# Second layer's attention values: from f32 products and key sums to three f16 products of halves, in a new order

## The reference

```python
latent_kv = x @ w_kv_down                       # rank 128
k, v = split(latent_kv @ w_kv_up); q = x @ w_q
att = softmax(where(causal, q k^T / 8, -inf))   # per head, 512 keys
y = einsum('bhqk,bkhd->bqhd', att, v)
return y.reshape(...) @ w_out
```

## Time and profile before

| | |
|---|---|
| runs shown | 3177.04, 3189.1, 3196.51 us (median 3189.1) |
| profiled execution | 3176.99 us, span 3175.3 us |
| busy share of the span | PE 94%, DVE 71%, ACT 56%, POOL 41% |
| granted TensorE clock, mean | 0.987 of 2.4 GHz |

### The profile page before, as it was taken

The page is one execution under the profiler, slowest core; times in us unless marked ns, Lnnn a source line. Parts: engine busy times, 40 slices in busy tenths (PEclk is TensorE's granted clock), DMA queues, the critical chain, the costliest instruction groups (busy, mean ns, idle before and its releaser), DMA issues.

```text
span 3175.3 us, 62002 instructions
## 1 busy us (share of the span) xinstructions
PE 2998.4 (94%) x22724; PEld 1597.1 (50%) x22724; DVE 2243.0 (71%) x4069; ACT 1765.3 (56%) x3674; POOL 1316.9 (41%) x1223
## 2 busy tenths in 40 slices
PE   4999999999999995799999999999999999999997
PEld 2565555555555553344444444444444444444443
DVE  4666666666666663787787787778778778878774
ACT  2666666665566664555555555555555555555543
POOL 1333333333333331354545545545544554455453
PEclk9999999999999998899999999999999999999998
DMA  4222222222222222434444445444444444453442
GB/s 119 51 53 51 51 51 56 64 56 63 51 51 51 62 50 83 110 100 117 128 113 123 116 115 135 111 112 126 115 121 112 128 126 104 125 135 100 124 121 67
DMA packets 271901, 297.58 MB, mean 94 GB/s; under 512 B 30832, under 2 KB 235760, under 8 KB 271088
## 3 DMA queue, kind: packets, MB, share of 16 engines
q1 hardware_dynamic: 249936, 276.88, 34.2%
q10 hardware_dynamic: 21664, 16.73, 1.7%
HBM read 141.46 MB, written 25.69 MB: 53 GB/s over the span
## 4 chain that ended last, share of the span: by engine, by line
PE 50%; DMA 3%; DVE 3%; issue 2%; SPq 2%; ACT 1%; POOL 0%; DVEq 0%; ACTq 0%; POOLq 0%
PE l_ps_out L1569 8%; PE l_ps_any L1469 6%; PE l_ps_any L1471 6%; PE l_ps_any L1470 6%; PE l_ps_any L1594 5%; PE l_ps_exp L1552 4%; PE l_ps_exp L1554 4%; PE l_ps_any L1601 4%; PE l_ps_any L1527 3%; DMA l_y_rec<-rec_scratch 2%; PE l_ps_sum L1580 2%; PE l_ps_exp L1556 2%; SPq L1099 1%; DVE l_neg_max L1392 1%; PE l_ps_any L1532 1%
## 5 line engine op out<-in xcount | busy, mean ns | idle before, releaser
L614 DVE TENSOR_REDUCE neg_max<-ps_any 128x1 f32<-128x384 f32 (+3 forms) x704 | 417.7, 636 | 264.0 <-PE ps_any L728 259.5
L1186 POOL TENSOR_TENSOR l_hid<-l_hid,l_spread 128x512 f32<-128x512 f32 x256 | 328.3, 1282 | 652.0 <-DVE l_hid L1421 481.1
L1273 ACT ACTIVATE l_probs<-l_ps_exp 128x512 f32<-128x512 f32 x640 | 376.8, 595 | 212.3 <-PE l_ps_exp L1556 201.8
L501 ACT ACTIVATE probs<-ps_exp 128x512 f32<-128x512 f32 x640 | 349.2, 602 | 151.5 <-PE ps_exp L743 150.8
L442 POOL TENSOR_SCALAR_AFFINE_SELECT probs<-probs 128x512 f32<-128x512 f32 x256 | 160.0, 637 | 591.1 <-ACT probs L501 591.1
L1392 DVE TENSOR_REDUCE l_neg_max<-l_ps_any 128x2 f32<-128x768 f32 (+2 forms) x384 | 316.3, 863 | 36.1 <-PE l_ps_any L1532 35.1
L1552 PE MATMUL l_ps_exp<-l_q_a,l_k_a 128*128 128x512 f16 (+3 forms) x1024 | 306.4, 300 | 10.0 <-DMA l_q_b<-l_max_row 6.3
L1569 PE MATMUL l_ps_out<-l_probs,l_v 128*64 128x512 f32 (+3 forms) x2048 | 303.9, 439 | 0.7 <-ACT l_yT L1248 0.7
L1425 DVE TENSOR_TENSOR l_hw<-l_hid,l_hw 128x512 f16<-128x512 f32 x272 | 258.6, 955 | 59.4 <-ACT l_hw L1256 58.9
L1554 PE MATMUL l_ps_exp<-l_q_b,l_k_b 65*128 65x512 f16 (+3 forms) x1024 | 295.3, 300 | 0.0
L1279 ACT ACTIVATE l_hid<-l_ps_any 128x512 f32<-128x512 f32 x272 | 162.4, 597 | 234.8 <-PE l_ps_any L1471 217.5
(11 more groups left out here) (233 smaller groups left out, 6514.4 us busy)
## 6 DMA issues: line engine op xcount, KB each, us to landing
l_spread<-route_scratch SPq DMA_DIRECT2D x128, 512.0 KB, 4.7
l_q_a<-l_q_hi SPq DMA_DIRECT2D x256, 128.0 KB, 2.4
l_y_rec<-rec_scratch SPq DMA_DIRECT2D x128, 256.0 KB, 4.3
l_q_b<-l_q_lo SPq DMA_DIRECT2D x128, 128.0 KB, 2.4
l_k_a<-l_k_hi SPq DMA_DIRECT2D x128, 128.0 KB, 3.0
l_k_a<-l_k_lo SPq DMA_DIRECT2D x128, 128.0 KB, 2.7
l_k_b<-l_k_hi SPq DMA_DIRECT2D x128, 128.0 KB, 2.7
q_st<-rot_hi SPq DMA_DIRECT2D x64, 128.0 KB
```

The source lines that it names most:

```text
L501: nc.scalar.activation(probs[:, n % 2, u], ps_exp[:, (10 * g + u) % 3], ACT.Exp, scale=float(HD0 + DR) ** -0.5).then_inc(exp_done.sem, 1)
L614: nc.vector.tensor_reduce(neg_max[:, n % 2, heads[0]:heads[0] + k, t], src, AX.X, ALU.max, negate=True).then_inc(drained["dve"], 1)
L1186: nc.gpsimd.tensor_tensor(at, at, spread[:, c % 3, n % SPREAD], ALU.mult).then_inc(weighted.sem, 1)
L1273: nc.scalar.activation(probs[:, n % 2, u], ps_exp[:, (5 * p + u) % ST_BANKS], ACT.Exp, scale=float(HD1) ** -0.5).then_inc(exp_done.sem, 1)
```

## The change

- Probabilities: for each unit ACT takes the exponential of the bank twice, to f16 (`probs` part 0) and to f32 (`p_in`, three slots); POOL subtracts, to f16 (`probs` part 1). The bank is free after the second. The scores get a constant added (`P_SHIFT` times `SHIFT` in a further row of the factors), and v a factor `V_SCALE`, which ACT takes out again.
- v: ACT writes the f16 hi half, DVE the lo half (`low_part`), and the bank is now counted as emptied by DVE.
- `values`: per key block three f16 products (hi*hi, hi*lo, lo*hi) for each of the two heads.
- `key_sum` and its POOL steps are gone. `sums` multiplies ones (f16) with both halves of the probabilities: 28 products a pair. Which queries share a row group of `ps_sum` changes (`HALVES`: blocks 0 and 3, 1 and 2), and `divide` becomes two instructions.
- `ORDER1` is another order of the same steps.

Unchanged lines are left out but for one ahead of each edit, and indents are cut; of the old order one line stands.

```diff
@@ -825,7 +825,11 @@
 XW, LW = X_SCALE * W_SCALE, LAT_SCALE * W_SCALE
-K_B = HD1 + 1
+K_B = HD1 + 2
+P_SHIFT = 0.13
+V_SCALE = 16.0
+P_SLOTS = 3
+HALVES = ((0, 3), (1, 2))
@@ -844,40 +848,40 @@
 ORDER1 = (
-    ("v", 0, 2, 0), ("rec", -1, 1), ("sums", -1, 7), ("exp", 0, 0, 4), ("v", 0, 3, 0), ("exp", 0, 1, 0),
...
+    ("spread_in", 0, 3), ("max", 0, 1, 1), ("exp", 0, 1, 0), ("max", 0, 1, 2), ("exp", 0, 1, 1),
+    ("max", 0, 1, 3), ("hw", 0, 4), ("rec_in", -1, 2), ("exp", 0, 1, 2), ("max", 0, 1, 4), ("hw", 0, 5),
+    ("values", 0, 0), ("exp", 0, 1, 3), ("up_in", 0, 6), ("exp", 0, 1, 4), ("turn_max", 0, 1), ("qk", 0, 2, 0),
+    ("qk", 0, 2, 1), ("gate_in", 0, 7), ("qk", 0, 2, 2), ("sums", 0, 0), ("divide", -1, 4), ("spread_in", 0, 4),
+    ("qk", 0, 2, 3), ("hw", 0, 6), ("v", 0, 0, 1), ("exp", 0, 2, 0), ("spread_in", 0, 5), ("rec_in", -1, 3),
+    ("max", 0, 2, 0), ("exp", 0, 2, 1), ("up_in", 0, 7), ("divide", -1, 5), ("down", 0, 0), ("exp", 0, 2, 2),
+    ("gate_in", 0, 8), ("hw", 0, 7), ("max", 0, 2, 1), ("down", 0, 1), ("up_in", 0, 8), ("max", 0, 2, 2),
+    ("gate_in", 0, 9), ("divide", -1, 6), ("values", 0, 1), ("max", 0, 2, 3), ("divide", -1, 7),
+    ("exp", 0, 2, 3), ("exp", 0, 2, 4), ("sums", 0, 1), ("norm", 1), ("spread_in", 0, 6), ("up_in", 0, 9),
+    ("gate_in", 0, 10), ("exp", 0, 3, 0), ("max", 0, 2, 4), ("exp", 0, 3, 1), ("load", 1), ("sums", 0, 2),
+    ("up_in", 0, 10), ("gate_in", 0, 11), ("turn_max", 0, 2), ("spread_in", 0, 7), ("up_in", 0, 11),
+    ("exp", 0, 3, 2), ("scale", 1), ("hw", 0, 8), ("out", -1, 1), ("v", 0, 1, 1), ("qk", 0, 3, 0),
+    ("v", 0, 2, 1), ("xnT", 1), ("hw", 0, 9), ("exp", 0, 3, 3), ("hw", 0, 10), ("qk", 0, 3, 1),
+    ("gate_in", 0, 12), ("exp", 0, 3, 4), ("values", 0, 2), ("up_in", 0, 12), ("hw", 0, 11), ("exp", 0, 4, 0),
+    ("gate_in", 0, 13), ("qk", 0, 3, 2), ("exp", 0, 4, 1), ("outT", -1), ("gate", 1), ("rec", 0, 0),
+    ("exp", 0, 4, 2), ("route", 1), ("qk", 0, 3, 3), ("exp", 0, 4, 3), ("sums", 0, 3), ("hw", 0, 12),
+    ("values", 0, 3), ("exp", 0, 4, 4), ("up_in", 0, 13), ("down", 0, 2), ("gate_in", 0, 14), ("exp", 0, 5, 0),
+    ("max", 0, 3, 0), ("v", 0, 3, 1), ("hw", 0, 13), ("exp", 0, 5, 1), ("up_in", 0, 14), ("max", 0, 3, 1),
+    ("rec_out", 0, 0), ("rec_in", 0, 0), ("exp", 0, 5, 2), ("gate_in", 0, 15), ("values", 0, 4),
+    ("max", 0, 3, 2), ("max", 0, 3, 3), ("hw", 0, 14), ("lat", 1), ("divide", 0, 0), ("cT", 1),
+    ("rec_in", 0, 1), ("sums", 0, 4), ("max", 0, 3, 4), ("divide", 0, 1), ("up_in", 0, 15), ("exp", 0, 5, 3),
+    ("gate_in", 0, 16), ("v", 1, 0, 0), ("turn_max", 0, 3), ("spread_in", 1, 0), ("qk", 1, 0, 0), ("hw", 0, 15),
+    ("qk", 1, 0, 1), ("exp", 0, 5, 4), ("up_in", 0, 16), ("exp", 0, 6, 0), ("gate_in", 1, 0), ("qk", 1, 0, 2),
+    ("up_in", 1, 0), ("qk", 1, 0, 3), ("exp", 0, 6, 1), ("sums", 0, 5), ("max", 1, 0, 0), ("exp", 0, 6, 2),
+    ("gate_in", 1, 1), ("exp", 0, 6, 3), ("spread_in", 1, 1), ("max", 1, 0, 1), ("hw", 0, 16), ("values", 0, 5),
+    ("exp", 0, 6, 4), ("up_in", 1, 1), ("gate_in", 1, 2), ("max", 1, 0, 2), ("down", 0, 3), ("exp", 0, 7, 0),
+    ("divide", 0, 2), ("divide", 0, 3), ("up_in", 1, 2), ("exp", 0, 7, 1), ("max", 1, 0, 3), ("values", 0, 6),
+    ("gate_in", 1, 3), ("max", 1, 0, 4), ("up_in", 1, 3), ("hw", 1, 0), ("exp", 0, 7, 2), ("gate_in", 1, 4),
+    ("spread_in", 1, 2), ("sums", 0, 6), ("qk", 1, 1, 0), ("hw", 1, 1), ("turn_max", 1, 0), ("hw", 1, 2),
+    ("hw", 1, 3), ("v", 1, 1, 0), ("exp", 0, 7, 3), ("up_in", 1, 4), ("qk", 1, 1, 1), ("exp", 0, 7, 4),
+    ("res", 0), ("out", 0, 0), ("v", 1, 2, 0), ("gate_in", 1, 5), ("exp", 1, 0, 0), ("up_in", 1, 5),
+    ("qk", 1, 1, 2), ("qk", 1, 1, 3), ("v", 1, 3, 0), ("exp", 1, 0, 1), ("gate_in", 1, 6), ("exp", 1, 0, 2),
+    ("sums", 0, 7), ("max", 1, 1, 0), ("exp", 1, 0, 3), ("rec_out", 0, 1), ("exp", 1, 0, 4), ("values", 0, 7),
+    ("rec", 0, 1),
@@ -944,7 +948,7 @@
 w_d = sb("w_d", [P, 2, EXPERTS, D], F16)
-ones_in = sb("ones_in", [P, SET, 32])
+ones_in = sb("ones_in", [P, SET, 32], F16)
@@ -965,11 +969,11 @@
 k_b = sb("k_b", [P, 2, G, T], F16)
-v = sb("v", [P, TB, H * HD1])
+v = sb("v", [P, TB, 2, H * HD1], F16)
 max_row = sb("max_row", [G * TB, 2, P], F16)
-probs = sb("probs", [P, 2, 5, T])
-key_sum = sb("key_sum", [P, G, T])
+probs = sb("probs", [P, 2, 2, 5, T], F16)
+p_in = sb("p_in", [P, P_SLOTS, T])
@@ -990,7 +994,7 @@
-flat = probs[:].rearrange("p s u t -> p (s u t)")
+flat = probs[:].rearrange("p s c u t -> p (s c u t)").bitcast(F32)
@@ -1001,7 +1005,7 @@
 program = layer1_program(batches)
-banks = Banks(program, filled_by1, filled_by1, lambda step: step[0] in ("v", "gate", "cT", "turn_max"))
+banks = Banks(program, filled_by1, filled_by1, lambda step: step[0] in ("gate", "cT", "turn_max"))
@@ -1027,7 +1031,9 @@
 exp_done = sig("exp_done", 5)
-added = sig("added", 4)
+p_ok = sig("p_ok", 5)
+p_lo_ok = sig("p_lo_ok", 5)
+v_hi_ok = sig("v_hi_ok", 2 * TB)
@@ -1071,6 +1077,8 @@
 split_late = [(w_g, w_g_in), (w_u, w_u_in), (w_d, w_d_in)]
+v_steps = [step[2:] for step in program if step[:2] == ("v", 0)]
+V_COUNT = {x: k + 1 for k, x in enumerate(v_steps)}
@@ -1100,7 +1108,7 @@
 emptied(sp, f"turn_max{b}_{n}")
-sp.dma_start(q_b[HD1:K_B, n % 2], max_row[:, n % 2]).then_inc(row_in.sem, 16)
+sp.dma_start(q_b[HD1:HD1 + 1, n % 2], max_row[:, n % 2]).then_inc(row_in.sem, 16)
@@ -1156,26 +1164,11 @@
-p = PAIRS * b + n
-s = key_sum[:, 2 * (n % 2):2 * (n % 2) + 2]
-u = probs[:, n % 2]
-if step[3] == 3:
-    if p >= 2:
-        pool.wait_ge(summed.sem, summed.at(p - 1, 0))
-    pool.wait_ge(exp_done.sem, exp_done.at(p, 4))
-    release(pool, pool_passed)
-    nc.gpsimd.tensor_copy(s[:, :, 0:P], u[:, 0:2, 0:P]).then_inc(added.sem, 1)
-    nc.gpsimd.tensor_tensor(s[:, :, P:T], u[:, 0:2, P:T], u[:, 2:4, 0:3 * P], ALU.add
-                            ).then_inc(added.sem, 1)
-if step[3] == 4:
-    pool.wait_ge(exp_done.sem, exp_done.at(p, 5))
-    pool.wait_ge(added.sem, added.at(p, 2))
-    nc.gpsimd.tensor_tensor(s[:, :, 2 * P:T], s[:, :, 2 * P:T],
-                            u[:, 4].rearrange("p (h q) -> p h q", h=2), ALU.add
-                            ).then_inc(added.sem, 1)
-    pool.wait_ge(added.sem, added.at(p, 3))
-    nc.gpsimd.tensor_tensor(s[:, :, 3 * P:T], s[:, :, 3 * P:T], u[:, 2:4, 3 * P:T], ALU.add
-                            ).then_inc(added.sem, 1)
+p, u = PAIRS * b + n, step[3]
+m = 5 * p + u
+pool.wait_ge(p_ok.sem, p_ok.at(p, u + 1))
+nc.gpsimd.tensor_tensor(probs[:, n % 2, 1, u], p_in[:, m % P_SLOTS], probs[:, n % 2, 0, u],
+                        ALU.subtract).then_inc(p_lo_ok.sem, 1)
@@ -1237,15 +1230,15 @@
     act.wait_ge(pv_done.sem, pv_done.at(PAIRS * (b - 1) + SET * half + SET, 0))
-nc.scalar.activation(v[:, n, half * T:half * T + T], full(act, f"v{b}_{n}{half}"), ACT.Copy,
-                     scale=1.0 / LW).then_inc(drained["act"], 1)
+nc.scalar.activation(v[:, n, 0, half * T:half * T + T], full(act, f"v{b}_{n}{half}"), ACT.Copy,
+                     scale=V_SCALE / LW).then_inc(v_hi_ok.sem, 1)
 act.wait_ge(pv_done.sem, pv_done.at(PAIRS * b + n, 1))
-nc.scalar.activation(yT[:, n], ps_out[:], ACT.Copy).then_inc(y_ok.sem, 1)
+nc.scalar.activation(yT[:, n], ps_out[:], ACT.Copy, scale=1.0 / V_SCALE).then_inc(y_ok.sem, 1)
@@ -1268,10 +1261,16 @@
     act.wait_ge(pv_done.sem, pv_done.at(p - 1, 0))
-    act.wait_ge(added.sem, added.at(p - 1, 0))
+    act.wait_ge(summed.sem, summed.at(p - 1, 0))
 act.wait_ge(exp_full.sem, exp_full.at(p, u + 1))
-nc.scalar.activation(probs[:, n % 2, u], ps_exp[:, (5 * p + u) % ST_BANKS], ACT.Exp,
-                     scale=float(HD1) ** -0.5).then_inc(exp_done.sem, 1)
+m = 5 * p + u
+bank = ps_exp[:, m % ST_BANKS]
+nc.scalar.activation(probs[:, n % 2, 0, u], bank, ACT.Exp, scale=float(HD1) ** -0.5
+                     ).then_inc(exp_done.sem, 1)
+if m >= P_SLOTS:
+    act.wait_ge(p_lo_ok.sem, m + 1 - P_SLOTS)
+nc.scalar.activation(p_in[:, m % P_SLOTS], bank, ACT.Exp, scale=float(HD1) ** -0.5
+                     ).then_inc(p_ok.sem, 1)
@@ -1286,8 +1285,9 @@
 nc.vector.memset(k_b[HD1:P], SHIFT).then_inc(prep, 1)
+nc.vector.memset(q_b[HD1:P], P_SHIFT).then_inc(prep, 1)
 nc.vector.memset(ones_in[:], 0.0).then_inc(prep, 1)
-dve.wait_ge(prep, 2)
+dve.wait_ge(prep, 3)
@@ -1373,6 +1373,10 @@
     low_part(f"xnT{b}", xn_p[:, b % 2, 1], xn_p[:, b % 2, 0], X_SCALE, x_hi_ok, x_hi_ok.at(b, 1))
+if name == "v":
+    half = step[3]
+    low_part(f"v{b}_{n}{half}", v[:, n, 1, half * T:half * T + T], v[:, n, 0, half * T:half * T + T],
+             V_SCALE / LW, v_hi_ok, v_hi_ok.at(b, V_COUNT[n, half]))
@@ -1406,8 +1410,12 @@
 dve.wait_ge(rec_in.sem, rec_in.at(p // 2, 32))
-y = yT[:, n].rearrange("p (f q) -> p f q", f=2)
-nc.vector.tensor_tensor(y, y, y_rec[:, :, n % 2], ALU.mult).then_inc(y_div.sem, 1)
+y = yT[:, n].rearrange("p (c q) -> p c q", q=P)
+for f, (c, d) in enumerate(HALVES):
+    part = y[:, c:d + 1:d - c]
+    ins = nc.vector.tensor_tensor(part, part, y_rec[:, f, n % 2].rearrange("p (c q) -> p c q", q=P),
```

(40 more changed lines are left out.)

33 lines of the change are left out of this document (removed).

## The result

The changed kernel is slower: 3,262.4 us median of four runs (3,256.7 to 3,269.0) against 3,189.6 us of the kernel before (3,177.0 to 3,196.5), a ratio of 1.0239 [1.0220, 1.0259]. The forecast was 3,180 us, with a range of 3,130 to 3,250. The profiled execution took 3,268.95 us, span 3,267.2; the one of before took 3,177.0.

What follows compares the result with a forecast made beforehand. The prediction took PE to bound the layer: -2.5 us of PE work + 1.7 of new waits = -0.8 a batch, x 15.5 = -12, +3 for the ends, gave 3168 against 3177.0, or 3180 at the median; range 3130 to 3250.

Steps and rivals of the forecast that it cites:

- Values and sums: PE's products: values gain 4.2 us a batch, sums lose 1.5, shape changes add 0.2; together -2.5.
- rival 3: Column tiles do not overlap in f16 on PE: +8 us a batch, about 3310 us; chance 3%.
- ACT and POOL at nothing: ACT's second reads (to 87 us a batch) and POOL's subtractions (to 71) cost PE nothing within the batch.
- POOL's blocking of DVE: DVE's two-SBUF-operand instructions stand until POOL's running one ends: 7.2 us a batch rises to 13.3, DVE to 105.
- Reciprocal steps and row "at nothing": SP's reciprocal write and read cost nothing; the row of maxima's transfer up to 0.5 us a batch.
- the 1.7: New PE waits a batch, in us, where DVE falls behind in emptying the four shared banks.
- the forecast's own range: 0 to 3 us of new waits a batch and the bounds of the sums: 3150 to 3210 us.
- rival 2: DVE becomes the bound: a batch of 119 us, +3.4 each, 3233 us or 3245 at the median; chance 25%.
- the 5 that I gave as its sign: PE's waits above 5 us a batch with DVE named would show rival 2.

Runs made afterwards that it cites:

- e8: e3 without ACT's second read of each exp bank (POOL subtracts from a constant): 3,204.2 us, 1.0061 to the kernel before.
- e1: The changed kernel's instructions in the order of before, with three sums steps moved earlier: 3,356.1 us, 1.0544 to the kernel before.
- e10: e3 with POOL's subtractions cut from 512 to 16 columns, the products reading the high half twice: 3,163.7 us, 0.9931 to the kernel before.
- e5: The changed kernel with only the second reciprocal read moved behind the row of maxima on SP's queue: 3,207.9 us, 1.0082 to the kernel before.
- e3: The changed kernel with only the first exp of pair 6, which needs the row of maxima, moved later: 3,200.5 us, 1.0061 to the kernel before.
- e13: e3 with the divide multiplying by a constant, so DVE doesn't stand for the reciprocals' read, still issued by SP: 3,170.6 us, 0.9957 to the kernel before.
- e9: e3 without v's low half on DVE, and with v's banks emptied by ACT alone: 3,213.9 us, 1.0104 to the kernel before.
- e14: e13 with POOL's subtractions also cut to 16 of 512 columns, as in e10: 3,152.3 us, 0.9904 to the kernel before.
- e7: The changed kernel with the moves of e3 and e5 together and five more moves to smooth DVE's steps: 3,234.9 us, 1.0162 to the kernel before.

## Why the prediction was wrong

**Values and sums: right, and a little better.** 1.75 us a pair, where the forecast's 1.68 and the 0.09 of the shape change make 1.77; the 0.03 in it for a first weight load is in no row, before or after. The column tiles overlap (rival 3 is out). The sums were mis-sized: less the 0.09, 0.57 us in place of 0.67, near the lower end of 0.55. The loss is 0.09 a pair and not 0.19. PE's work fell by 3.4 us a batch at full clock; the forecast had 2.5. By the Trainium skill ("TensorE: Matmul & The Clock Gate", LDWEIGHTS, with "TensorEngine Tiling (Array Packing)", Restrictions) 28 loads one after another were an estimated 0.75 us; the trace has 0.66 from the first product to the next shape, so the loads do not cost that one after another, and the measurement decides.

**ACT and POOL at nothing on PE's path: right in the new order.** No wait of PE names them, e8 shows the second read to be free, and e1 shows the cover: in the old order they are the two largest waits. ACT's total was too high, 87 us a batch against 81, since the reads overlap; POOL's 71 came out at 70.

**POOL's blocking of DVE: the mechanism right, its growth wrong.** The forecast let it rise from 7.2 to 13.3 us a batch, with hw's mean above 1,050 ns. It fell. Over the 1,500 us, half of hw's instructions take 681 ns or less and half of the divides 418 or less, which is what they take alone; with the batch's means of 847 and 598 ns, 17 and 16 of them lose 5.7 us, less than before the change, and DVE has 96 us of work and not 105. In the trace the 113 hw subtractions that began while POOL did nothing took 672 to 693 ns, the 96 that began during POOL's subtraction 1,019 on average and up to 1,570: the mechanism stands, but the order dodges POOL more than a random overlap would. The 37 us of e10 are what all of the subtraction costs in this order, not its growth over the key sums; the kernel before had more blocking and waited 1.5 us a batch. So this step, which I called decisive, was not the one that failed.

**Reciprocal steps and row "at nothing": the step that failed.** I wrote that SP stands for one landing, "but nothing that it queues behind them is due for several steps", and gave the row "up to 0.5 us a batch, inside the 1.7". I saw the write and the read, and missed the second read behind them: it waits for the divides, they wait for the first read, and the row stands behind all of it. The landing of 1.7 us is right where no such read is ahead, and then the cover that I counted is enough (e5); behind the read's 2 x 256 KB it was 3.6 to 5.0. The row's wait was 2.5 us a batch, and the clock made it more: some 60 us by e3, 50 by e5. The same step made DVE stand at the divide: 30 us more by e13. Either alone is more than the 9 us by which the forecast lay under the kernel before. With the row's wait taken away the change stands at 3,200 (by the ratio 3,209), just inside the forecast's own range of 3,150 to 3,210, but still not faster; with both taken away (e13) it is at 0.9957, some 13 us faster. So this one term, put at nothing, is enough to make up the miss. Taking POOL's subtraction away gets as far (e10, 0.9931), but POOL's blocking had its price in the forecast, and the reads had none.

**A part of that agreement is luck.** In e13 the period is 0.8 us under the kernel before, and the forecast had -0.8. But it is made of -3.4 of work and +2.6 of waits, where the forecast had -2.5 and +1.7: two errors of 0.9 us cancel. Two sums in the forecast are off besides, and neither decides: a batch of 119 us is 3.1 over 115.9, not the 3.4 of rival 2, and the bounds given for the own range would let it begin near 3,140 and not at 3,150.

**Rival 2 came near the time, by another way.** DVE is named in 6.3 us a batch, above the 5 that I gave as its sign. But DVE is not the bound: it is busy 1,184.6 of the 1,500 us, before 1,185.7. It is late, at two places, and then waits itself. Taking 5.4 us of its work away (e9, with v's banks back on ACT) gained nothing; taking its stand away (e13) did.

**What stays open.** In e14 PE still waits 3.4 us a batch, against 1.5 before, nearly all of it for DVE. Which order would hide that was not found; e7 was the one attempt. And how the gain of e13 and that of e10 overlap is shown only in their sum.

## What to carry to other kernels

When an order moves a step that a queue issues in sequence, follow that queue from the step to the next urgent transfer and write down what each entry waits for: a wait that is harmless in itself is paid by whatever stands behind it. Take a small transfer's landing time from a place where the queue is as full as it will be. And test an order apart from the work: the old work in the new order showed in one run that the wait for the row belongs to it.

## What the runs showed of the hardware

- Behind the wait of 2.63 us the 512-column products ran 0.43 us apart, the 1.2 GHz level, for about 3 us, from 0.9 us after the restart. The 8 us around them have a granted clock of 0.79. From 1500 to 3000 us such stretches cost 1.6 us a batch on top of the waits (112.5 us of work against 110.8 in e13 at a clock of 1.00).
- 28 f16 products of 128 or 256 columns, each with its load, on four 32-column tiles: 0.66 us, 24 ns each, the shape change in it.
- A POOL subtraction of 128x512 with one f16 and one f32 input takes 1.17 us; the f32 multiplication beside it 1.27 to 1.33.
- The row of 4 KB lands after 1.7 us as a rule; right behind two transfers of 256 KB on its queue it took 3.6 to 5.0 us in all 13 batches, and 1.7 again in e5, where they are issued behind it. A few rows of the other groups took 2.3 to 3.5 us with no transfer of the program's ahead of them still under way; why is open.
